# Attention over 2048 positions, 32 heads: projections product by product at four steps of a head, and one score product with a wider mask for the own chunk of a key tile

## What is computed

```python
q = x @ W_q;  k = x @ W_k;  v = x @ W_v
latent = (k + v) @ W_down_kv
k_rec = heads(latent @ W_up_k);  v_rec = heads(latent @ W_up_v)
scores = einsum('bhqd,bhkd->bhqk', heads(q), k_rec) / sqrt(d)
decay = exp(-0.01 * abs(t[:, None] - t[None, :]))      # t: position
attn = softmax(scores * decay)
out = einsum('bhqk,bhkd->bhqd', attn, v_rec) @ W_o
```

## Time and profile before

| | us |
|---|---|
| median of 3 runs (lowest, highest) | 1645.92 (1645.17, 1649.04) |
| the profiled execution's time | 1644.78 |
| its span, first to last instruction | 1643.1 |
| attention's exps, first to last | 101.0 to 1111.0 |
| a pair of heads with projections | 63.40 |
| a pair of heads without | 59.82 |

### The profile page before, as it was taken

The page is one execution under the profiler, slowest core; times in us unless marked ns, Lnnn a source line. Parts: engine busy times, 40 slices in busy tenths (PEclk is TensorE's granted clock), DMA queues, the critical chain, the costliest instruction groups (busy, mean ns, idle before and its releaser), DMA issues. The chain is left out here.

```text
span 1643.1 us, 26430 instructions
## 1 busy us (share of the span) xinstructions
PE 1553.8 (95%) x8752; PEld 685.6 (42%) x8753; DVE 558.6 (34%) x1624; ACT 1121.3 (68%) x1330; POOL 58.6 (4%) x104
## 2 busy tenths in 40 slices
PE   7769999999999999999999999987999999999996
PEld 5523333333333333333333333333646556556554
DVE  5612323313323323223222122132453543444442
ACT  4459999999999999999999999982222223223210
POOL 1000000000000000000000000000000000000000
PEclk9879999999999999999999999997999999999998
DMA  7565664575466466456556446522010010001000
GB/s 190 206 145 130 165 129 128 134 157 130 118 156 147 109 147 161 112 129 161 107 134 143 95 104 132 119 51 78 27 39 13 26 38 13 26 15 37 1 13 15
DMA packets 105425, 163.42 MB, mean 99 GB/s; under 512 B 52080, under 2 KB 72304, under 8 KB 96928
## 3 DMA queue, kind: packets, MB, share of 16 engines
q1 hardware_dynamic: 105376, 162.83, 41.1%
HBM read 120.84 MB, written 41.94 MB: 99 GB/s over the span
## 5 line engine op out<-in xcount | busy, mean ns | idle before, releaser
L702 ACT ACTIVATE work<-ps 128x1024 f32<-128x1024 f32 x1024 | 951.3, 1084 | 68.9 <-DVE ps L536 36.4
L632 PE MATMUL ps<-work 128*32 128x512 f32 x4096 | 548.1, 607 | 0.0
L624 PE MATMUL ps<-Q_st,K_st 64*128 64x512 f32 (+3 forms) x2432 | 440.9, 430 | 43.0 <-ACT work L702 28.2
L624 PEld LDWEIGHTS ps<-Q_st,K_st 64*128 64x128 f32 x2432 | 230.9, 184 | 541.5 <-ACT work L702 450.5
L536 DVE TENSOR_TENSOR ps<-ps,small 128x128 f32<-128x128 f32 x512 | 153.5, 300 | 743.0 <-PE ps L624 741.4
L1816 PE MATMUL ps<-xT,stack 128*128 (+1 forms) x320 | 156.7, 612 | 1.5 <-PEq L455 1.5
L1824 PE MATMUL ps<-xT,stack 128*128 (+1 forms) x320 | 151.3, 595 | 0.0
L1839 PE MATMUL ps<-stack,work 128*128 128x256 f32 x640 | 141.3, 380 | 0.0
L1789 ACT ACTIVATE work<-ps 128x512 f32<-128x512 f32 x80 | 47.6, 595 | 135.4 <-PE ps L1816 135.3
L632 PEld LDWEIGHTS ps<-work 128*32 128x32 f32 x4096 | 80.9, 108 | 113.7 <-issue 87.7
L1839 PEld LDWEIGHTS ps<-stack,work 128*128 128x128 f32 x640 | 120.4, 190 | 16.0 <-issue 0.2
(11 more groups left out here) (115 smaller groups left out, 746.7 us busy)
## 6 DMA issues: line engine op xcount, KB each, us to landing
K_st<-halves_dram SPq DMA_DIRECT2D x256, 256.0 KB, 5.6
halves_dram<-work SPq DMA_DIRECT2D x64, 512.0 KB, 3.7
Q_st<-halves_dram SPq DMA_DIRECT2D x256, 128.0 KB, 5.6
work<-in_L_attn_x SPq DMA_DIRECT2D x16, 512.0 KB, 4.9
attn_dram<-work SPq DMA_DIRECT2D x16, 256.0 KB, 6.6
work<-attn_dram SPq DMA_DIRECT2D x8, 512.0 KB, 3.9
out<-work SPq DMA_DIRECT2D x8, 512.0 KB, 2.9
decay<-in_c_decay SPq DMA_DIRECT2D x8, 256.0 KB, 10.4
```

Of the source, the lines that this page charges most:

```text
L624: m = nc.tensor.matmul(ps[:, half_of(s, half) + c % 2, q0 % CH:q0 % CH + w], K_st[tile, par, a, s * P:(s + 1) * P], Q_st[tile, par, a, at: ...
L632: m = nc.tensor.matmul(ps[STRIP * c:STRIP * (c + 1), ACC + par], Vg[:, par, s], probs[:, probs_of(par, s), chunk(c)], start=s == 0, stop=s ...
L702: nc.scalar.activation(probs[:, probs_of(par, s), half * HALF:(half + 1) * HALF], src, ACT.Exp, scale=SCALE).then_inc(s_["exp_done"], 1)
```

## The change

Two edits, with what they pull along.

The projection is issued product by product: `project` takes k, and the two products of the first one stand at s = 6 and 8, those of the second at s = 11 and 13. `prepare` moves to s = 9, 10, 11 and to s = 14, 15 and s = 0 of the second head.

The own chunk of a key tile is no longer cut at the tile's first query: all its 512 queries are computed with FALL, and the mask mends the queries below the tile too. So it covers (s % 4 + 1) x 128 columns, and a mask of 512 columns (`wide`) is loaded in place of the two of 128 columns.

```diff
--- before.py
+++ after.py
@@ -104,6 +104,11 @@
     return v
 
 
+def wide_mask(small):
+
+    return carve(small, 400, CH)
+
+
 def diagonal_masks(small):
 
     return carve(small, 1840, P), carve(small, 1968, P)
@@ -209,8 +214,7 @@
             for r in range(P // STRIP):
                 for sign in range(2):
                     sp.dma_start(decay[STRIP * r:STRIP * (r + 1), sign, :], io["c_decay"][sign]).then_inc(dec_in, 16)
-            for mask, dst in enumerate(diagonal_masks(small)):
-                sp.dma_start(dst, io["c_diag"][mask]).then_inc(dec_in, 16)
+            sp.dma_start(wide_mask(small), io["c_wide"]).then_inc(dec_in, 16)
             for n in range(4, NB):
                 load_block(n)
             for k in range(2 * QC):
@@ -222,7 +226,7 @@
             sp.wait_ge(xn_ready, NB)
             load_halves(sp, K_st, Q_st, halves_dram, 0, 0, stack_in)
             sp.wait_ge(w_in, 6 * 16)
-            sp.wait_ge(dec_in, 10 * 16)
+            sp.wait_ge(dec_in, 9 * 16)
             sp.wait_ge(stack_in, 16 * HALVES_DMAS)
 
         @block.gpsimd
@@ -282,7 +286,7 @@
                     nc.vector.tensor_copy(w_veff, ps[:, 3, :].rearrange("p (k n) -> p k n", k=KD)).then_inc(eff_sb, 1)
                 if n >= 3:
                     if n == 3:
-                        dve.wait_ge(dec_in, 10 * 16)
+                        dve.wait_ge(dec_in, 9 * 16)
                     prepare(n - 3)
             for k in range(NB - 3, 2 * QC):
                 prepare(k)
@@ -379,7 +383,7 @@
     att = carve(work, 11776, KT, 2 * HD)
     split = carve(work, 12288, 2, CH)
     part = carve(work, 13312, 2, 2, 2, CH)
-    dmask, _ = diagonal_masks(small)
+    wide = wide_mask(small)
     rden = carve(small, 256, CT, QC)
     bound = carve(small, 928, 2)
     bound_new = carve(small, 930, 2)
@@ -405,21 +409,10 @@
     PREPS = 2 * (NPAIR - PPU)
     chunk = lambda c: slice(c * CH, (c + 1) * CH)
 
-    def cut(lo, hi):
-
-        while lo < hi:
-            end = min(hi, (lo // CH + 1) * CH)
-            yield lo, end
-            lo = end
-
     def score_pieces(kt, half):
 
-        a, z = half * HALF, (half + 1) * HALF
-        own = kt * P
-        for lo, hi in cut(a, min(z, own)):
-            yield lo, hi - lo, RISE
-        for lo, hi in cut(max(a, own), z):
-            yield lo, hi - lo, FALL
+        for c in range(half * (QC // 2), (half + 1) * (QC // 2)):
+            yield c * CH, CH, RISE if c < kt // CT else FALL
 
     def half_of(s, half):
 
@@ -438,11 +431,9 @@
 
         return n * NSTEP + (s - 1 if par == 0 and s < 2 else s - 2)
 
-    def own_block(s):
-
-        at = s * P % HALF
-        bank = half_of(s, s * P // HALF) + at // CH
-        return ps[:, bank, at % CH:at % CH + P]
+    def own_chunk(s):
+
+        return ps[:, half_of(s, s * P // HALF) + s * P % HALF // CH, 0:(s % CT + 1) * P]
 
     def pairs(eng, pair):
         pair(0, True, True, False)
@@ -533,7 +524,7 @@
             def mask(n, s):
 
                 wait(dve, "sc_ps", n * NHALF + 2 * s + s * P // HALF + 1)
-                nc.vector.tensor_tensor(own_block(s), own_block(s), dmask, ALU.mult).then_inc(s_["masked"], 1)
+                nc.vector.tensor_tensor(own_chunk(s), own_chunk(s), wide[:, (CT - 1 - s % CT) * P:], ALU.mult).then_inc(s_["masked"], 1)
 
             def prepare(piece, c, which, k, bank):
 
@@ -585,10 +576,12 @@
                             copy_sums(n - 1, 1 - par)
                         if s == 5 and not (first and par == 0):
                             normalise(n - 1, 1 - par)
-                        if prep and par == 0 and s >= 8 and s < 11:
-                            prepare(s - 8, it % PPU, 0, 2 * it, idle)
-                        if prep and par == 0 and s >= 12 and s < 15:
-                            prepare(s - 12, it % PPU, 1, 2 * it + 1, idle)
+                        if prep and par == 0 and s >= 9 and s < 12:
+                            prepare(s - 9, it % PPU, 0, 2 * it, idle)
+                        if prep and par == 0 and s >= 14:
+                            prepare(s - 14, it % PPU, 1, 2 * it + 1, idle)
+                        if prep and par and s == 0:
+                            prepare(2, it % PPU, 1, 2 * it + 1, idle)
                         if last and par:
                             if s == 7:
                                 set_flag()
@@ -609,11 +602,11 @@
             first_block["tensor_start"](pe)
             prime(pe, *"proj_ps sc_ps pv_done oT_ps".split())
 
-            def project(at, which, bank):
-                for k in range(KD):
-                    m = nc.tensor.matmul(ps[:, bank], w_unit[:, which, k], xT[:, k, at:at + CH] if isinstance(at, int) else xT[:, k, bass.ds(at, CH)],
-                                         start=k == 0, stop=k == KD - 1)
-                m.then_inc(s_["proj_ps"], 1)
+            def project(at, which, bank, k):
+                x = xT[:, k, at:at + CH] if isinstance(at, int) else xT[:, k, bass.ds(at, CH)]
+                m = nc.tensor.matmul(ps[:, bank], w_unit[:, which, k], x, start=k == 0, stop=k == KD - 1, skip_group_check=True)
+                if k == KD - 1:
+                    m.then_inc(s_["proj_ps"], 1)
 
             def scores(par, n, s, half):
                 wait(pe, "exp_done", halves_done(n, s, half))
@@ -658,14 +651,18 @@
                             transposes(n - 1, 1 - par)
                         if par == 0 and prep:
                             at = ((it // PPU + 1) // KD) * S + (it % PPU) * CH
-                            if s == 7:
+                            if s == 6:
                                 wait(pe, "w", it + 1)
                                 if not first:
                                     wait(pe, "att_sb", n)
-                                project(at, 0, idle)
+                                project(at, 0, idle, 0)
+                            if s == 8:
+                                project(at, 0, idle, 1)
                             if s == 11:
                                 wait(pe, "proj_free", 2 * it + 1)
-                                project(at, 1, idle)
+                                project(at, 1, idle, 0)
+                            if s == 13:
+                                project(at, 1, idle, 1)
                         if end:
                             if s == 7:
                                 wait(pe, "att_sb", n)
@@ -1903,10 +1900,12 @@
     decay = np.exp(np.array([-DECAY, DECAY])[:, None, None] * np.broadcast_to(t, (STRIP, S)))
     s, q = np.arange(P)[:, None], np.arange(P)[None, :]
     diag = np.where(s > q, np.exp(-2 * DECAY * (s - q)), 1.0)
+    rel = np.arange(CH)[None, :] - (CH - P)
+    wide = np.where(s > rel, np.exp(-2 * DECAY * (s - rel)), 1.0)
     sel = np.zeros((NE, HT - NSH, P))
     for e in range(NE):
         sel[e, e // EPT, (e % EPT) * MR:(e % EPT + 1) * MR] = 1.0
-    out = {"c_ident": np.eye(P), "c_decay": decay, "c_diag": np.stack([diag, diag.T]), "c_sel": np.tile(sel.reshape(NE, -1)[:, ::2], (3, 1)) * BF16_ONES,
+    out = {"c_ident": np.eye(P), "c_decay": decay, "c_diag": np.stack([diag, diag.T]), "c_wide": wide, "c_sel": np.tile(sel.reshape(NE, -1)[:, ::2], (3, 1)) * BF16_ONES,
            "c_iota": np.tile(np.arange(NE), (P, 1))}
     return {k: np.ascontiguousarray(v, dtype=np.float32) for k, v in out.items()}
```

## The result

The changed kernel takes 1657.24 us (median of 4 runs, 1656.48 to 1659.35) against 1646.14 before: ratio 1.0071, 95% interval 1.0059 to 1.0083. It is 11 us slower; the prediction had 19, in a range of 1654 to 1674. The spans of the profiled executions are 1654.7 and 1643.1.

A forecast was written before the change was run, and what follows sets the result against it. ScalarE's exps were taken to bound the attention. Eleven pairs at 1.48 us (16.3), first pair 1.05, three plain pairs 0.6 and last head 1.0 gave +19 us, hence 1665 us, 1.2% slower; range 1654 to 1674.

The forecast's parts named there:

- What bounds the kernel: Attention part: ScalarE's exps, one every 0.917 us, set the pace; time moves only where an exp starts late.
- Slack: Lateness an exp tolerates: a step's first exp 1.14 us, 0.81 behind a 128-column mask; its second 0.62, or 0.29.
- Rival A: Single products of the projections hide in the slack, making the kernel faster: 1618 us; chance 0.12.
- The rule: An insertion makes TensorE late; what exceeds the slack of the exp is lost.
- Single products: Projection insertions: 1.49 us between scores, 1.08 late each, with the change between 64-row and 128-row products paid four times a pair.
- the upper bound: Single-product insertion: 1.67 us between scores, if each record took its mean of 0.62 and did not overlap the next.
- Wider masks: Masks between scores and exp take 0.30, 0.43, 0.56 and 0.69 us, shrinking slack; about 0.2 us a plain pair.
- Uncut chunks: worth 0: Fewer score products on TensorE: saved work is hidden under ScalarE, worth 0.
- VectorE late behind piece 0: `prepare`'s first piece holds VectorE 1.41 us behind a mask; step 15 loses 0.26, the turn of the head 0.75.
- The sum: Whole kernel: +1.48 us for each of eleven pairs with projections, together +19 us, giving 1665 us.
- the last head: Final head, where ScalarE waits for masks: widening at steps 10, 11, 13 and 14 goes in in full, 1.0 us.
- Rivals B and C: B: 1.30 us between scores and masks 0.05 cheaper, 1654 us; C: masks 0.10 dearer, 1674 us; chance 0.12 each.

The follow-up runs named there:

- the masks and uncut chunks alone: Changed kernel with `project` and `prepare` as before, so only the uncut own chunk and masks of 128 to 512 columns are new: 1648.12 us, ratio 1.0017.
- the change with cut chunks: Changed kernel with the own chunk still cut and the wide mask with ones in front of the block: 1662.29 us, ratio 1.0094 against the kernel before.
- the single product left in the kernel: Kernel before with only the first product of each projection, at steps 7 and 11 (output differs): 1624.06 us, ratio 0.9873.
- the order of the halves: Half holding the own chunk goes first in steps 8 to 15: in the kernel before 1637.56 us, in the changed kernel 1642.35 us.
- the split alone: Kernel before with projections product by product at steps 6, 8, 11 and 13, `prepare` moved, masks and score products as they were: 1651.3 us, ratio 1.0043.
- the projections at 9 and 13: Kernel before with own half first and projections of two products at steps 9 and 13: 1634.82 us; with uncut chunks and wide masks too: 1634.79 us.

## Why the prediction was right, and where it was too high

**What bounds the kernel.** Right. Every kernel's time follows the holes of ScalarE: twelve times the change of a pair with projections and four times that of a plain one give the totals, e.g. 12 x (61.68 - 63.40) = -20.6 against 1624.06 - 1644.25 = -20.2. In most kernels this comes within 1 us; the masks and uncut chunks alone are 3 us above that sum and the change with cut chunks 2 above, the change itself 2 below.

**Slack.** Right, and shown on its own by the single product left in the kernel (61.68 against 61.7) and by the order of the halves (62.88 against 62.8, 63.25 against 63.3 to 63.4). Rival A falls with the first. The rule is good to about 0.2 us a pair: the split alone (64.01 against 63.8) and the projections at 9 and 13 (62.65 against 62.4 to 62.5) came out dearer by that.

**Single products.** Right: 1.49 us between scores, and the split costs 0.5 to 0.6 a pair with narrow masks or with the own half first (1.0 to 1.1 with wide masks in order, see below). Each further visit costs 0.27 of TensorE's time, 0.54 for the two more of a pair. That each changes the tiling mode twice, to 128 rows and back, and that a change drains TensorE, is the Trainium skill's rule (TensorEngine Tiling (Array Packing), Key Properties); these rows go the same way, by four changes more a pair where the prediction counted two, but no run separates a drain from the rest of the 0.27. The mean of 0.62 for a record, which gave the upper bound, was not approached.

**Wider masks.** Durations right to 0.01. Width costs 0.17 a pair alone (rule: 0.2) and 0.63 behind single products (64.64 against 64.01). What each place of a pair loses, read from ScalarE's timelines: a hole with 0.11 added, or what a run of exps takes over 1.02 us for its first and 0.917 for each further one.

| place, us lost | predicted for the change | split, narrow, cut | split, wide, cut | the change |
|---|---|---|---|---|
| step 7 | 1.09 | 0.73 | 1.13 | 1.12 |
| run to step 9 | 0.19 | 0.57 | 0.17 | 0.16 |
| step 9 | 0.98 | 0.90 | 1.03 | 0.98 |
| run to step 12 | 0.37 | 0.00 | 0.11 | 0.11 |
| step 12 | 0.42 | 0.80 | 0.68 | 0.66 |
| run to step 14 | 0.06 | 0.11 | 0.11 | 0.06 |
| step 14 | 1.11 | 0.85 | 1.12 | 1.11 |
| step 15 | 0.26 | 0.01 | 0.00 | 0.01 |
| turn to the second head | 0.75 | 0.52 | 0.66 | 0.64 |
| second head | 0.20 | 0.02 | 0.26 | 0.22 |
| turn to the next pair | 0.70 | 0.80 | 0.68 | 0.69 |
| sum | 6.13 | 5.31 | 5.95 | 5.76 |

The larger hole at step 7 is not where the width costs its 0.6. What the 512-column mask takes there (0.40 more) a narrow mask loses just behind, in the run to step 9 (0.40 less): TensorE is late by the same amount, and it is only lost earlier. The width is paid at step 9 (0.13) and step 14 (0.27), where a single product meets a mask of 256 and of 384 columns in front of a second exp, and these are the 0.13 and 0.27 by which those masks are longer than one of 128; the turn to the second head adds 0.14, and the second head and the turn behind it 0.12. Blocks of two products at 7 and 11 are felt at steps 8 and 12, whose masks have 128 columns in either kernel. So the width costs little there, and the split and the masks together cost 0.4 more than each by itself.

**Uncut chunks: worth 0.** This was wrong, and small: 0.21 a pair in the changed kernel, 0.24 with narrow masks, 0.16 unsplit. The reasoning held for paced steps, where TensorE waits anyway. But a pair with projections spends most of its first head catching up, and there a saved product can come back as an earlier exp: the last two columns of the table differ by 0.01 to 0.05 in most places, which fits this but does not show it product by product. I had seen the 1.66 us of a cut step and taken it for the uncut one too; why a plain pair gains 0.08 as well, though TensorE waits in most of its steps, no row here shows in detail.

**VectorE late behind piece 0.** This term was mis-sized. I held VectorE for 1.41 us behind a mask (626.04 to 627.45). VectorE's timeline in the changed kernel, mask of step 14, piece 0, mask of step 15:

```profile
645.39 0.57 DVE L527 TENSOR_TENSOR ps<-ps,small 128x384 f32<-128x384 f32 x1 [2.47 <-PE ps L617]
645.87 0.68 DVE L537 TENSOR_TENSOR work<-ps,decay 128x512 f32<-128x512 f32 x1
646.47 0.68 DVE L538 TENSOR_TENSOR work<-ps,decay 128x512 f32<-128x512 f32 x1
647.06 0.69 DVE L527 TENSOR_TENSOR ps<-ps,small 128x512 f32<-128x512 f32 x1
```

The mask of step 14 ends at 645.39 + 0.57 = 645.96 and that of step 15 starts at 647.06: 1.10. In the row of before piece 0 began 0.12 behind its 0.30 us mask; here it begins 0.09 before the end of the longer one, and the next mask 0.09 before the end of piece 0. Step 15 therefore loses nothing, where I had 0.26 (3 exps in 2.86 us, 194.98), and the turn of the head 0.53 + 0.11 = 0.64 and not 0.75. At steps 10 to 12 the sum was right, 0.11 + 0.55 + 0.11 = 0.77 against 0.79, but its parts were not: less at 10 and 11, more at 12.

**The sum.** 1.48 a pair was computed, 1.03 measured. With the chunks cut it is 1.24, so 0.21 is the uncut chunks. The other 0.24 are VectorE's two terms, 0.35 too high (step 15 and the turn to the second head, the predicted column against that of the split with wide masks on cut chunks), of which TensorE's terms and the second head took 0.17 back; 0.06 more come from the kernel before, whose pair is that much longer than the prediction's terms make it (58.69 for 64 exps at 0.917 and 4.65 lost, against 63.40). Eleven pairs make 5 us of it, the last head 0.7 (+0.3 for 1.0: holes before wide masks there did grow, but work behind them took some of it back), and the profiled execution happened to start its attention 1.6 us early. That is nearly all of the 8 us between 1665 and 1657. Rivals B and C lay below and above it: B's 1.30 between scores and its cheaper masks are refuted, though its total came nearer than mine. It is in part luck that 1657 lies in the range: its ends were B and C, and neither happened. The two terms that brought the time down, VectorE's hold and the uncut chunks, had no bounds in it.

## What to carry to other kernels

Before a long insertion into a paced pipeline is cut up, work out the slack of each consumer, one by one: pieces longer than the smallest slack lose together as much as the whole (a pair loses 1.86 us to one product of each projection, 3.58 to two in one piece, 4.19 to two apart), and each visit pays its 0.27 us again. Ask also which mask each piece will meet: the same masks cost 0.2 us a pair behind blocks and 0.6 behind single products, since these meet the wider ones. Here the smallest slack belonged to the exp that had a mask in front of it and came second; changing the order of two halves gave 6.5 us, and with it uncut chunks with wide masks cost nothing on balance (62.75 us a pair against 62.88). With the projections at 9 and 13 or with uncut chunks it is 8 to 9 us (1635 to 1637 against 1644). And a saved instruction on an engine that waits is not worth nothing in every step: with the halves in order the uncut chunks gained 0.16 to 0.24 us in a pair with projections, and 0.08 in a plain one, though TensorE waits in most steps there.

## What the runs showed of the hardware

A visit of 128-row products between 64-row scores costs TensorE 0.27 us beyond its records: with the same 96 records the group takes 54.0 us in 48 visits and 47.6 in 24. VectorE's multiply from PSUM to PSUM takes as long as from PSUM to SBUF (0.70 for 128 x 512, against 0.69 in the earlier trace rows). Two VectorE instructions in a row overlap by 0.08 to 0.09 us in the rows above. Behind a short mask it depends on what went before: piece 0 started 0.12 us after the end of a mask of 0.30 us that VectorE had waited for, but piece 1, in the kernel before, 0.10 us before the end of the 0.30 us mask at 627.45, for which it had not waited:

```profile
627.65 0.68 DVE L549 TENSOR_REDUCE small<-ps 128x1 f32<-128x512 f32 x1
```

So the same piece held VectorE 1.41 us behind a mask of 0.30 us and 1.10 behind one of 0.57. That a longer mask hides what piece 0 has to do before it starts would explain it, but is not shown.
